# Normalisation of four parts moved into the tail of the part ahead, a band check moved into the loop, answers added by two engines, and one scan for the tile sums

## The reference

```python
x = x + mamba_and_ffn(layernorm(x))       # selective scan over 256 steps, then a feed-forward
x = x + moe0(layernorm(x))                # 8 experts, 2 per token, relu
x = x + linear_attention(layernorm(x))    # softmax-free: x times a 128 x 128 sum
x = x + moe1(layernorm(x))                # 8 experts, 2 per token, silu(x wg) * (x wu)
x = x + decay_attention(layernorm(x))     # 16 heads of 8, a penalty that grows with distance
x = x + deep_network(layernorm(x))        # 8 experts of three layers, combined by a gate
x = x + window_attention(layernorm(x))    # rotary, keys within a window
x = x + last_feed_forward(layernorm(x))   # ternary weights, four layers
def _layernorm(x, axis=-1, eps=1e-05):
    m = jnp.mean(x, axis=axis, keepdims=True)
    v = jnp.var(x, axis=axis, keepdims=True)
    return (x - m) / jnp.sqrt(v + eps)
```

## Time and profile before

| | |
|---|---|
| runs | 1405.73, 1405.86 (median), 1406.10 us |
| profiled execution | 1409.14 us, its span 1407.4 us |
| PE busy | 1111.0 us (79% of the span) |
| PE weight loads | 716.8 us (51%) |
| DVE busy | 902.3 us (64%) |
| ACT busy | 679.7 us (48%) |
| POOL busy | 546.3 us (39%) |

### The profile page before, as it was taken

The page is one execution under the profiler, slowest core; times in us unless marked ns, Lnnn a source line. Parts: engine busy times, 40 slices in busy tenths (PEclk is TensorE's granted clock), DMA queues, the critical chain, the costliest instruction groups (busy, mean ns, idle before and its releaser), DMA issues. The chain is left out here.

```text
span 1407.4 us, 25102 instructions
## 1 busy us (share of the span) xinstructions
PE 1111.0 (79%) x8340; PEld 716.8 (51%) x8349; DVE 902.3 (64%) x3013; ACT 679.7 (48%) x1256; POOL 546.3 (39%) x675
## 2 busy tenths in 40 slices
PE   8877677779278653199946999959995999899998
PEld 3322223227178643199934777734333777654544
DVE  3499889995545456367549988843858778850200
ACT  2685556544134301132216888637664888641221
POOL 6188978772734314544433222010013655110000
PEclk9988999999589855599968999979996999999999
DMA  2999000000522206211120000020002000000000
GB/s 60 161 191 164 0 0 1 0 1 8 183 61 58 90 13 211 61 43 45 35 72 1 2 3 2 3 54 3 1 0 85 3 3 2 3 2 0 15 0 15
DMA packets 80456, 58.31 MB, mean 41 GB/s; under 512 B 14043, under 2 KB 69222, under 8 KB 80327
## 3 DMA queue, kind: packets, MB, share of 16 engines
q1 hardware_dynamic: 74630, 45.20, 15.3%
q0 software_dynamic: 4544, 9.38, 1.8%
q10 hardware_dynamic: 1152, 2.10, 0.4%
HBM read 28.13 MB, written 28.52 MB: 40 GB/s over the span
## 5 line engine op out<-in xcount | busy, mean ns | idle before, releaser
L713 PE MATMUL bank<-hC,ident 128*128 128x512 f32 x256 | 135.9, 656 | 45.3 <-POOL hC L998 43.1
L998 POOL TENSOR_TENSOR hC<-h,Cs 128x1024 f32<-128x1024 f32 x64 | 150.6, 2353 | 47.3 <-DVE h L897 47.0
L897 DVE TENSOR_TENSOR_SCAN h<-bank,state,dBx 128x512 f32<-128x512 f32 x128 | 157.3, 1270 | 3.5 <-POOL dBx L991 1.5
L1381 POOL DMA_INDIRECT moe_answers<-moe_yw,moe_xg x78 | 83.8, 1075 | 132.9 <-DVE moe_yw L1558 74.2
L2547 DVE CUSTOM_DVE_ANT_0 decay_below<-bank,decay_q_mask 128x256 bf16<-128x256 f32 x256 | 97.5, 418 | 16.9 <-PE bank L2360 16.1
L713 PEld LDWEIGHTS bank<-hC,ident 128*128 128x128 f32 x256 | 46.9, 201 | 109.0 <-POOL hC L998 68.7
L2547 DVE CUSTOM_DVE_ANT_0 window_below<-bank,window_q_mask 128x192 bf16<-128x192 f32 x256 | 80.4, 353 | 29.3 <-PE bank L2360 27.7
L810 ACT ACTIVATE bank<-dt,A 128x512 f32<-128x512 f32 x128 | 83.2, 683 | 27.1 <-DVE h L897 25.6
L2488 ACT ACTIVATE decay_pb<-bank 128x512 f32<-128x512 f32 x128 | 76.2, 598 | 34.5 <-PE bank L2375 34.0
L1452 PE MATMUL bank<-moe_xgT,moe_wac 128*128 128x128 f32 x624 | 87.4, 286 | 6.4 <-issue 4.1
L1467 PE MATMUL bank<-moe_wd,moe_hT 128*128 x624 | 83.0, 277 | 5.2 <-DVE moe_hT L1545 2.5
(11 more groups left out here) (478 smaller groups left out, 2823.8 us busy)
## 6 DMA issues: line engine op xcount, KB each, us to landing
moe_slots<-blank SPq DMA_DIRECT2D x16, 1040.0 KB, 17.7
moe_xg<-moe_slots SPq DMA_DIRECT2D x78, 65.0 KB, 1.9
moe_wa<-in_moe_w SPq DMA_DIRECT2D x2, 2048.0 KB
moe_back<-moe_answers SPq DMA_DIRECT2D x8, 256.0 KB, 5.6
moe_back<-moe_answers ACTq DMA_DIRECT2D x8, 256.0 KB, 5.9
moe_wu<-in_moe_wu SPq DMA_DIRECT2D x1, 2048.0 KB
deep_w<-in_deep_w SPq DMA_DIRECT2D x3, 512.0 KB
moe_answers<-moe_yw,moe_xg POOLq DMA_INDIRECT x78, 2.5
```

The costliest lines, as they stand in the source:

```text
L713: last = nc.tensor.matmul(sum_bank(hh)[:], k.ident[:], hC[:, u % 2, hh, :], start=(n == 0), stop=(n == NS - 1))
L897: v.tensor_tensor_scan(h[:, u % 2, hh, :], decay_bank(u, hh)[:], dBx[:, u % 2, hh, :], state[:, n, hh:hh + 1], ALU.mult, ALU.add).then_inc ...
L998: g.tensor_tensor(hC[:, u % 2], h[:, u % 2], Cs[:, u % 2, None, :].to_broadcast([P, H, CW]), ALU.mult).then_inc(q_hC, 1)
L1381: nc.gpsimd.indirect_dma_start(answers, bass.IndirectOffsetOnAxis(index, 0), yw[:, i % NY, :], None)\
```

## The change

1. The objects `Norm` of linear attention, decay attention, deep network, window attention and last feed-forward are made at the program's start, and the tail of `experts` takes the one of the part behind it. In the tail of moe0: statistics and power of chunk 0 of linear attention. In the tail of moe1 (`full`): all five steps of chunk 0 of decay attention.
2. Linear attention now does rows of chunk c, then statistics of chunk c + 1, and so on. In decay attention the statistics of the 12 tiles stand behind the splits of tiles 0 and 1.
3. The loop of decay attention gets a `NormAhead` with the same places as `last`, for chunks 0 to 2 of the deep network, which writes its transposed rows to `blank`. The deep network starts with three gates; only chunk 3 is normalised there. ACT no longer waits for all three weights ahead of its first step.
4. The tail of `experts`: POOL adds the pairs of chunks 1 and 3, DVE those of 0 and 2.
5. The running sum is one `tensor_tensor_scan`.
6. The band check stands in the loop, at y = 11 and 12. POOL copies `X` to `X0` and adds the bias to `X` in place, in two instructions where one was; `add` reads and writes `X`. The path for all keys, which is not run here, normalises again.

```diff
@@ class Norm / NormAhead
+class NormAhead:
+    TURNS = {(15, 2): 0, (15, 5): 1, (16, 0): 2}
+    STATS = {(14, 0): 0, (14, 3): 1, (14, 6): 2}
+    ROWS = {(15, 0): 0, (15, 3): 1, (15, 6): 2}
+    TAKES = {(15, 3): 0, (15, 6): 1, (16, 0): 2}
...
+    def vector_step(self, dve, y, w):
+        if (y, w) in self.STATS:
+            dve.wait_ge(self.added, (self.STATS[y, w] + 1) * CT)
+            self.norm.stats(dve, self.STATS[y, w])
+        if (y, w) in self.ROWS:
+            self.norm.rows(dve, self.ROWS[y, w])
+
+    def pool_end(self, pool):
+        for c in range(self.k.C - 1):
+            self.norm.power(pool, c)
...
@@ experts
+                pool.wait_ge(s_back[1], 16 * 2)
+                nc.gpsimd.tensor_tensor(back[:, 1, 0], back[:, 1, 0], back[:, 1, 1], ALU.add).then_inc(s_sum_odd, 1)
+                after.power(pool, 0)
+                pool.wait_ge(s_back[3], 16 * 2)
+                nc.gpsimd.tensor_tensor(back[:, 3, 0], back[:, 3, 0], back[:, 3, 1], ALU.add).then_inc(s_sum_odd, 1)
...
-                step(v.tensor_copy(ends[:, 0:1], tiles[:, 0:1]))
-                for e in range(1, E):
-                    step(v.tensor_tensor(ends[:, e:e + 1], ends[:, e - 1:e], tiles[:, e:e + 1], ALU.add))
+                step(v.tensor_tensor_scan(ends[:], k.ones[:, 0:E], tiles[:], 0.0, ALU.mult, ALU.add))
...
                 both(0)
-                for c in range(C):
-                    if c + 1 < C:
-                        both(c + 1)
-                    onto_x(c)
+                onto_x(0)
+                dve.wait_ge(s_x, 1)
+                after.stats(dve, 0)
+                both(2)
+                onto_x(1)
+                if full:
+                    after.rows(dve, 0)
+                onto_x(2)
+                onto_x(3)
@@ linear
-                k.norm_vector(L0, keep=rows)
+                for c in range(C):
+                    norm.rows(dve, c, keep=rows)
+                    if c + 1 < C:
+                        norm.stats(dve, c + 1)
@@ deep
-            turn(0)
+            for c in range(C - 1):
+                gate(c)
             for n in range(STEPS):
                 if n < units:
                     first(n)
-                if n + 1 < C:
-                    turn(n + 1)
-                if 0 <= n - 1 < C:
-                    gate(n - 1)
+                if n == 0:
+                    turn(C - 1)
+                if n == 1:
+                    gate(C - 1)
...
-            act.wait_ge(w_1, 32)
-            act.wait_ge(w_2, 32)
-            act.wait_ge(w_3, 32)
@@ softmax_mixer
+        def longest_of_all(pe):
+            pe.wait_ge(s_f, 1)
+            pe.wait_ge(s_qT, T)
+            for a in range(2):
+                last = nc.tensor.matmul(bank[6][0:1, a * P:(a + 1) * P], small[:, a:a + 1], k.ident[:], start=True, stop=True)
+            last.then_inc(s_f, 1)
...
+            if not windowed:
+                norm.stats(dve, 1)
             norm.rows(dve, 1)
...
-                    nc.gpsimd.tensor_tensor(X0[:], k.X[:], bo[:, None, :].to_broadcast([P, T, P]), ALU.add)\
+                    nc.gpsimd.tensor_copy(X0[:], k.X[:]).then_inc(s_x0, 1)
+                    pool.wait_ge(s_x0, 1)
+                    nc.gpsimd.tensor_tensor(k.X[:], k.X[:], bo[:, None, :].to_broadcast([P, T, P]), ALU.add)\
                         .then_inc(s_x0, 1)
```

More of the change, by code:

```diff
@@ L156, in norm_vector @@
[L156 to L170, removed]
-            self.nc.gpsimd.wait_ge(self.ln_ve, self.Q + h + 1)
-            self.norm_pow(h)
@@ new lines, in normalise_again, with _ @@
+def normalise_again(k, name, X, to, chunks):
+    a = Again(k, X, to, lambda n: k.sem(f"{name}_{n}"))
+    norm = Norm(a, tuple((c,) for c in range(chunks)))
+    with k.nc.Block() as block:
+        @block.gpsimd
+        def _(pool):
+            for c in range(chunks):
+                norm.power(pool, c)
+        @block.tensor
+        def _(pe):
+            for c in range(chunks):
+                norm.turn(pe, c, k.bank[7])
+        @block.scalar
+        def _(act):
+            for c in range(chunks):
+                norm.take(act, c, k.bank[7])
+        @block.vector
+        def _(dve):
+            for c in range(chunks):
+                norm.stats(dve, c)
+            for c in range(chunks):
+                norm.rows(dve, c)
@@ L1255, in scatter, with experts @@
                     .then_inc(self.s_sent, 16)
-def experts(k, r, early, first):
+def experts(k, r, early, after, full, first):
     nc, t, C, T, E = k.nc, k.t, k.C, k.T, k.E
@@ L1317, in experts @@
         y_read = s_yw if gated else s_yb
-        s_back, s_sum, s_x = [sem(f"back{c}") for c in range(C)], sem("sum"), sem("x")
+        s_back, s_sum, s_sum_odd, s_x = [sem(f"back{c}") for c in range(C)], sem("sum"), sem("sum_odd"), sem("x")
         hidden_done = s_u if gated else s_g
@@ L1428, in _ @@
                 fetch_answers(act, 1)
+                if full:
+                    after.take(act, 0, bank[7])
             @block.tensor
@@ L1483, in _ @@
                         down(i - 1)
+                if full:
+                    after.turn(pe, 0, bank[7])
             @block.vector
@@ L1635, in _ @@
             def _(pool):
+                for c in range(1, C):
+                    norm.power(pool, c)
                 nc.gpsimd.memset(half[:], -0.5).then_inc(s_h, 1)
-                k.norm_pool()
                 pool.wait_ge(s_h, 1)
@@ L1833, in gpsimd @@
             g = nc.gpsimd
-            for c in range(C):
-                norm.power(pool, c)
+            norm.power(pool, C - 1)
             g.memset(sel[:], 0.0).then_inc(s_sel, 1)
@@ L1998, in vector @@
             v_ = nc.vector
[L1999 to L2003 removed]
+            norm.stats(dve, C - 1)
+            norm.rows(dve, C - 1)
             for c in range(C):
@@ L2302, in softmax_mixer @@
             ahead.added = s_x
+        if not windowed:
+            bound = float(((P + 1 - EXP_IS_ZERO) / 2.0) ** 2)
+            flag = sb("flag", [1, 1], U32)
+            small, both_max = sb("small", [P, 2]), sb("both", [1, 4])
+            s_f = sem("flag")
+        FLAG_AT = T - 4
         inside = lambda y: 0 <= y < T
@@ L3052, in gpsimd @@
     def gpsimd(self, pool):
-        for c in range(self.k.C):
-            self.norm.power(pool, c)
+        self.norm.power(pool, self.k.C - 1)
     def pair(self, pe, n):
```

254 lines of the change are left out of this document (113 added, 141 removed).

## The result

The changed kernel took 1412.45 us (median of 4, 1408.56 to 1414.07) against 1405.88 for the one before: a ratio of 1.0046, 95% interval 1.003 to 1.0061. It is slower, by about 6.5 us. In a later session, beside 23 runs of the kernel before, the ratio was 1.004 (1.0027 to 1.0053).

The account below looks back on a forecast made before the run. The prediction took PE and DVE to bound decay attention's middle, and chains through five engines the heads and tails of the parts. Its terms summed to -3.4 us from 1405.86, forecasting 1402.4 us, range 1397 to 1407.5.

Parts of the forecast that it names:

- Table of moe1: In moe1, one scan replaces a copy and seven additions, so SP's first fetch comes earlier: -4.2 us; 0 in moe0.
- Tail of moe0: End of moe0: chunk 0's statistics precede DVE's last additions while two pair additions move to POOL, covered: +0.5 us.
- tail of moe1: End of moe1: DVE gains statistics and rows, loses two additions; the tail ends 2.2 us later.
- Head of linear attention: Start of linear attention: rows(0) goes earlier, but further chunks run statistics, power and rows in series: +0.8 us.
- Head of decay attention: Start of decay attention: first projection 3.8 us earlier, but rows(1) waits for 12 tiles' statistics and power: +2.3 us.
- X0 and the bias: In decay attention, POOL's two long instructions replace one and hold DVE a second time: +1.5 us.
- Band check and tail of decay attention: Decay attention's loop: band check steps cost PE +0.4 us; normalisation steps for the deep network add +2.9 us.
- Head of the deep network: Start of the deep network: chunks 0 to 2 are ready, so gates start 2.8 us in: -5.1 us.
- D: Rival: decay attention's steps at y = 14 to 16 cost 11.5 us, not 2.9, giving 1411 us; chance 0.08.
- B: Rival: heads give more, deep network gains 6.5 us, decay's tail costs +1; near 1399 us; chance 0.20.
- C: Rival: POOL's long X0 and bias instructions hold DVE longer, +4 instead of +1.5, giving 1406 us; chance 0.13.
- E: Rival: the scan doesn't move the first fetch, or loads still set the deep network's start; 1406.6 us; chance 0.11.

Follow-up runs that it names:

- early_drain: The changed kernel plus a POOL drain right after its last indirect DMA in each mixture of experts, ahead of its wait for the answers; 0.9971 of the kernel before.
- before_pool_late: The kernel before, plus POOL waiting for the last answers in both mixture-of-experts tails and then doing a small memset; 1.0062 of the kernel before, 8.7 us slower.
- mid_drain: The changed kernel plus a POOL drain after the 20th of 39 indirect DMAs in each mixture of experts, none at the loop's end; one trace, 1408.28 us.
- after: The first traced execution of the changed kernel, nothing further edited; 1408.56 us, the fastest of its four.

## Why the prediction was wrong

It forecast 1402.4 with 1397 to 1407.5; 1412.45 came. All four things that it named as signs of being right were there (the fetch 1.52 us behind the scatter, DVE's wait of 2.40 for the power, two long POOL instructions each beside a stretched one of DVE, gates from 2.0 us on), and none of its signs looked at how POOL ends a block. By its own steps, each against the trace:

- **Table of moe1**, -4.2: -3.3 to -3.9 in the two traces of the changed kernel, -3.0 as a time by itself. Right: the fetch goes by the scatters. It is a little smaller than the term, and in moe0 the fetch of the changed kernel moved by 0.3 us at most, near the 0 of the forecast.
- **Tail of moe0**, +0.5, and **tail of moe1**, +2.2: this is the step that failed. Taken from the first pair addition to the clearing of the semaphores, the tails grew by 5.1 (6.9 to 12.1) and 5.6 us (6.5 to 12.1). With the drain out of the way they grew by 0.45 and 2.4: the arithmetic in the step was right, and what was left out is the drain of POOL at the block's end. It had stood in the kernel before as well, 5.5 and 5.9 us long, and ended 6 us before the block did, so no view of busy time showed it. Work that waits for the answers, put ahead of it in POOL's program, moved it onto the path. The change put two additions and a power there, and 4.7 + 3.2 = 7.9 us came in, by the traces. The prediction priced POOL only for its additions (1.27 us each, taken as covered) and put what POOL must do behind its last instruction at nothing, without a reason.
- **Head of linear attention**, +0.8: -0.3 by the traces of the changed kernel, up to the copy to `lin_S`. The three trips to POOL are there, but rows(0) gave as much. In the traces where the clock stayed low it is +1.0.
- **Head of decay attention**, +0.1 behind the barrier (the rest of +2.3 was the tail): +0.6 to rows(1). Right in kind; the statistics and the power were on the path, and taking them off again gave 4.3 us at rows(1), and at tile 0 between traces with as many falls of the clock.
- **X0 and the bias**, +1.5: +2.5. The second hold was there (1.26 on the cast ahead of the 4.01). The term missed that PE's longer wait is followed by a lower clock (0.57 in the windows 779 to 783). With one instruction both were gone; by the table of falls the hold itself is 0.8 to 0.9 of it and the fall the rest. The Trainium skill's page "SBUF — State Buffer", section "Who interferes with whom", says that DVE contends with GpSimd for the shared ports in a two-port mode, and with two inputs in SBUF when GpSimd reads there, and that for the two-port modes whichever issues first holds the ports for its whole instruction while the other fully blocks. The trace agrees that DVE is stopped, in the loop (1.26 and 4.01) and in the tail of moe1 (rows 2.06 beside POOL's addition, 1.11 without).
- **Band check and tail of decay attention**, +0.4 and +2.9: +0.3 and +1.7. Right in kind, smaller.
- **Band check's block**, -2.5: -2.5.
- **Head of the deep network**, -5.1: -7.4, taken up to the first work of window attention. Right in kind, larger. The gates started 2.0 us behind the block's start, not 2.8, and from 954 on PE didn't stop again.

By the traces the terms without the drain come to about -6 (-3.6 + 0.45 - 0.3 + 2.4 + 0.6 + 2.5 + 2.0 - 2.5 - 7.4), so without it the forecast's sign would have held; early_drain, at 0.9971, is 4 us faster than before. With 7.9 for the drain the pieces give +2, and the times say +5.6 to +6.6. The first trace alone is a poor measure: it has one fall of the clock less than the second, and its piece up to the end of mamba was 349.1 us long, where before had 351.2 and the changed kernel and its edits, alike up to there, had 349.1 to 353.7. The second trace of the changed kernel (1413.68 us, the median of its session) and the one of before (1409.14, where before's median in that session was 1409.29) are the better pair. Of these the changed kernel's span is 4.2 us longer: +10.8 in the tails, +4.4 from there to tile 0 of decay attention, +2.0 in the loop's end, +0.3 in linear attention, -3.3 for the table, -2.5 for the check's block, -7.6 for the deep network. That is inside the interval of the ratio (3.8 to 7.5 us), so no remainder is left that the times could tell from none.

Of the rivals, D (slower, 1411) came near the time by luck: the steps at y = 14 to 16 cost 1.7 us, not 11.5. B was right on two pieces (the deep network gave more than its 6.5, the loop's end cost 1.7 where B had 1 and the forecast 2.9), and C had the right place with +4 where +2.5 came. E didn't occur.

## What to carry to other kernels

Before work is put at the end of an engine's program, look at what that engine does behind its last instruction and how long it was done before the barrier: an engine that looked idle can have been paying for something. A GpSimd that has issued indirect DMAs drains them at the block's end; if it gets work that waits, let it drain first, while it waits anyway. An instruction of GpSimd over a whole tensor in SBUF was cheap here for GpSimd only; DVE stood still for it, and PE's clock fell behind the stall. And before a piece of one trace is compared with that of another, compare their granted clocks: here 1.3 to 3 us of a piece came and went with them.

## What the runs showed of the hardware

- POOL's drain after indirect DMAs: 5.54 us behind POOL's last instruction in moe0 and 5.86 in moe1, the same to 0.02 us in all twelve traces whose drain was undivided, whether it stood behind a DMA, an addition or a memset; 0.06 to 0.08 without indirect DMAs since the last drain. Waiting doesn't shorten it: 9.60 us of waiting for the answers lay ahead of the memset in before_pool_late. It is cut by a drain in between (3.99 + 1.63), and goes by the number of indirect DMAs since the last one: 0.082 us for each, from 19 to 71 of them (mid_drain, after). What POOL does in this time no run shows.
- A stall of PE at 1.00 clock was followed by a stretch at the lower level with PE full (PEclk 0.57 in the window 779 to 783, 1.00 behind it), a second cost behind a stall that the stall's own length doesn't contain; it was 1.3 to 1.9 us for each fall in decay attention.
- The same program of linear attention (that of the changed kernel) took 41.2 to 42.1 us or 43.6 to 44.7 us, the latter at a mean granted clock of 0.54 (early_drain) against 0.64 (after). Why the clock rose early in some executions and not in others is open.
